# Two-layer graph attention: late mask blocks in two raw buffers with spread packs, and a preparation turned two steps behind its packing

## What is computed

```python
def _gat(x, adj, W_heads, a1, a2, W_out, b_out):          # first layer
    Wh = jnp.einsum('nf,hfd->hnd', x, W_heads)
    s1 = jnp.einsum('hnd,hd->hn', Wh, a1)
    s2 = jnp.einsum('hnd,hd->hn', Wh, a2)
    e = s1[:, :, None] + s2[:, None, :]
    e = jnp.where(e > 0, e, ALPHA * e)
    e = jnp.where(adj[None, :, :] > 0, e, NEG)
    att = jax.nn.softmax(e, axis=-1)
    hp = jax.nn.elu(jnp.einsum('hnm,hmd->hnd', att, Wh))
    feat = jnp.transpose(hp, (1, 0, 2)).reshape(N, NHEADS * NHID)
    return feat @ W_out + b_out
x = _layernorm(x + _L0_gnn_ref(...))                       # second layer: the same with 4 heads, no elu
x = _layernorm(x + _L1_gnn_ref(...))
```

## Time and profile before

| | us |
|---|---|
| median of 3 runs | 2948.03 (2943.8 to 2948.91) |
| the profiled execution | 2945.86, its span 2943.8 |
| preparation, to the first matmul of sweep 0 | 205.5 |
| sweeps 0 to 5, with the late units | 285.7 |
| PE busy over the span | 2739.7 (93%) |
| DVE, ACT, POOL busy | 1967.2 (67%), 2055.0 (70%), 571.0 (19%) |

### The profile page before, as it was taken

One profiled execution on the slowest core, in us unless ns is written; L12 is line 12 of the kernel. 1 busy time (PEld: TensorE's weight loads), 2 busy tenths in 40 slices (PEclk: granted clock), 3 DMA queues, 4 the chain that ended last, 5 costly groups with the idle time before them and its releaser, 6 DMA issues. The chain is left out here.

```text
span 2943.8 us, 62560 instructions
## 1 busy us (share of the span) xinstructions
PE 2739.7 (93%) x26702; PEld 2363.4 (80%) x26702; DVE 1967.2 (67%) x3079; ACT 2055.0 (70%) x3213; POOL 571.0 (19%) x447
## 2 busy tenths in 40 slices
PE   7986768999999999999999999999979959999997
PEld 3445656788888888888888888888868849999997
DVE  5345446877777767776777677675534458889887
ACT  4545556677777778777777877777732259999986
POOL 0021002632323323232323233130001150000000
PEclk9998989999999999999999999999989989999999
DMA  7983331111101111011011111000034344243230
GB/s 253 403 292 119 99 111 60 46 32 27 37 29 28 33 28 36 21 40 33 21 40 28 29 36 32 25 21 22 17 124 140 108 149 132 75 139 103 87 127 16
DMA packets 189144, 235.19 MB, mean 80 GB/s; under 512 B 13594, under 2 KB 113050, under 8 KB 188860
## 3 DMA queue, kind: packets, MB, share of 16 engines
q1 hardware_dynamic: 188868, 231.20, 24.4%
HBM read 180.49 MB, written 50.66 MB: 79 GB/s over the span
## 5 line engine op out<-in xcount | busy, mean ns | idle before, releaser
L419 PE MATMUL l_ps<-l_uv,l_bc 128*128 128x258 f16 x16384 | 1858.6, 275 | 85.8 <-DVE l_bc L649 81.7
L419 PEld LDWEIGHTS l_ps<-l_uv,l_bc 128*128 128x128 fp8e4 x16384 | 1602.6, 98 | 339.5 <-DVE l_bc L649 86.4
L503 ACT ACTIVATE l_bc<-l_s1b,l_kc 128x512 fp8e4<-128x512 f32 x2048 | 1281.9, 708 | 89.2 <-PE l_ps L419 89.1
L648 DVE SCALAR_TENSOR_TENSOR l_bc<-l_bc,mask_t 128x512 uint32<-128x512 uint32 x512 | 468.3, 915 | 412.5 <-ACT l_bc L503 410.0
L1016 PE MATMUL l_ps<-l_uv,l_bc 128*128 128x130 f16 x8192 | 490.9, 221 | 43.0 <-DVE l_bc L1290 41.1
L1016 PEld LDWEIGHTS l_ps<-l_uv,l_bc 128*128 128x128 fp8e4 x8192 | 485.9, 98 | 48.3 <-DVE l_bc L1290 46.7
L649 DVE TENSOR_TENSOR l_bc<-l_bc,mask_t 128x512 uint32<-128x512 uint32 x512 | 492.1, 961 | 0.0
L1109 ACT ACTIVATE l_bc<-l_s1b,l_kc 128x1024 fp8e4<-128x1024 f32 x432 | 453.4, 1141 | 0.7 <-PE l_ps L1016 0.5
L232 POOL TENSOR_TENSOR l_tu<-l_whx,l_eu 128x516 f32<-128x516 f32 x56 | 63.7, 1138 | 1225.8 <-PE l_ps L419 1223.9
L521 ACT COPY l_e<-l_ps 128x258 f32<-128x258 f32 x256 | 94.4, 369 | 260.9 <-PE l_ps L419 260.9
L654 DVE SCALAR_TENSOR_TENSOR l_e<-l_ps,l_sc,l_e 128x258 f32<-128x258 f32 x256 | 118.0, 481 | 162.0 <-ACT l_e L521 162.0
(11 more groups left out here) (152 smaller groups left out, 1399.6 us busy)
## 6 DMA issues: line engine op xcount, KB each, us to landing
l_uv<-in_adj SPq DMA_DIRECT2D x128, 512.0 KB, 6.7
l_uv<-uv SPq DMA_DIRECT2D x128, 260.0 KB, 5.4
l_s1b<-l_srow SPq DMA_DIRECT2D x64, 256.0 KB, 3.2
l_whx<-l_wh SPq DMA_DIRECT2D x64, 256.0 KB, 4.4
feat<-l_e SPq DMA_DIRECT2D x64, 256.0 KB, 2.4
l_uv<-feat SPq DMA_DIRECT2D x32, 512.0 KB, 3.7
l_wh<-l_bc SPq DMA_DIRECT2D x38, 256.0 KB, 8.0
uv<-l_uv SPq DMA_DIRECT2D x8, 1040.0 KB, 4.7
```

Of the source, the lines that this page charges most:

```text
L419: last = nc.tensor.matmul(sums(t, m), pattern(k, m).bitcast(F8)[:, j, t * P:(t + 1) * P], uv[:, slot(h, order[k]) + j, 2 * m * W1:2 * (m + ...
L503: ins = act.activation(pattern(k, 0).bitcast(F8)[:, j, :], s1b[q][:, :], ACT.Relu, bias=kc[:, h, jt:jt + 1], scale=STEEP, saturate=False)
L648: dve.scalar_tensor_tensor(c, v, ONE8X4, m, ALU.bitwise_xor, ALU.bitwise_and)
```

## The change

- Late units use two raw buffers in turn (`home(n)` is n % 2), and `load_unit(n)` waits for VectorE's pack of unit n-2 instead of n-1. Two loads are issued before sweep 0, then four in each sweep, for units two ahead.
- The packs of late units stand behind every second chunk of a sweep's eight turns (m = 1, 3, 5, 7: chunks 3, 5, 7 and the next sweep's chunk 1), on ScalarE and VectorE alike, instead of m = 1 to 4. The fourth stands right ahead of the copies of the sums.
- The second raw buffer takes the place of the four late pack buffers. Of four late units, the first two are now packed into a part of `mask_t` that is written last (4 rows of 512 bytes each), the others into the two pack buffers of preparation.
- In preparation `packed_at` begins with steps 0 and 1, so units 0 and 1 are packed on ScalarE after the copies of these steps and on VectorE ahead of `scores`; the other 38 are spread over steps 3 to 59. Every unit is turned and written two steps after its pack instead of one.
- The weights W, a1 and a2 are loaded ahead of the first part of x.

```diff
-    packed_at = [3 + n * 58 // EARLY for n in range(EARLY)]
+    packed_at = [0, 1] + [3 + n * 58 // (EARLY - 2) for n in range(EARLY - 2)]
+    turned_at = [i + 2 for i in packed_at]
...
-        late = [words[:, twin + RAW + r * PK:twin + RAW + (r + 1) * PK] for r in range(PER)]
+        late = [mask_t[:, at:at + 4, 7 * blk:8 * blk].rearrange("p (m a) (j k) -> p m a j k", m=2, k=2)
+                for at in (24, 28)]
...
+        def home(n):
+            return n % 4 if n < EARLY else n % 2
+
         def loads(n):
-            return 32 * (n // 4 + 1 if n < EARLY else EARLY // 4 + n - EARLY + 1)
-
-        def raw(n):
-            return raws[n % 4 if n < EARLY else 0].rearrange("p (m k j) -> p m k j", m=2, k=2)
+            return 32 * (n // 4 + 1 if n < EARLY else EARLY // 4 + (n - EARLY) // 2 + 1)
+
+        def raw(n, k):
+            return raws[home(n)].rearrange("p (m k a j) -> p m k a j", m=2, k=2, a=2)[:, :, k, :, :]
 
         def pair(n):
-            return (packs[n % 2] if n < EARLY else late[n % PER]).bitcast(U8).rearrange("p (m j k) -> p m j k", m=2, k=2)
+            if n >= EARLY and n % PER < 2:
+                return late[n % PER]
+            return packs[n % 2].bitcast(U8).rearrange("p (m a j k) -> p m a j k", m=2, a=2, k=2)
...
-                    sp.wait_ge(s_pd, n - 3 if n <= EARLY else n)
+                    sp.wait_ge(s_pd, n - 3 if n < EARLY + 2 else n - 1)
...
-            load_x(0)
             for k in range(KF):
                 sp.dma_start(wall[:, k, :, :], W[:, k * P:(k + 1) * P, :].rearrange("h p e -> p h e")).then_inc(s_wl, 16)
             for m, a in enumerate((a1, a2)):
                 sp.dma_start(abc[:, m, :, :], a.unsqueeze(0).to_broadcast([P, H, D])).then_inc(s_wl, 16)
-            for i in range(1, XPARTS):
+            for i in range(XPARTS):
...
-            n = EARLY
-            load_unit(n)
+            for n in range(EARLY, EARLY + 2):
+                load_unit(n)
...
-                if g < LATE:
-                    n += 1
+                ahead_of = range(EARLY + 2 + PER * g, min(EARLY + 2 + PER * (g + 1), UNITS))
+                for n in ahead_of[:1]:
                     load_unit(n)
                 if g > 0:
                     store(g - 1)
                     if g < G - 1:
                         load_mean(g + 1)
-                if g < LATE:
-                    for _ in range(PER - 1):
-                        n += 1
-                        if n < UNITS:
-                            load_unit(n)
+                for n in ahead_of[1:]:
+                    load_unit(n)
...
-                    if packed_at[n] + 1 == i:
+                    if turned_at[n] == i:
                         turn_unit(n)
...
-                act.wait_ge(s_ul[n % 4 if n < EARLY else 0], loads(n))
+                act.wait_ge(s_ul[home(n)], loads(n))
                 if 2 <= n < EARLY:
                     act.wait_ge(s_mt, n - 1)
-                if EARLY <= n < EARLY + PER:
-                    act.wait_ge(s_pd, EARLY)
+                elif EARLY <= n < EARLY + 2:
+                    act.wait_ge(s_pw, STEPS)
+                elif EARLY <= n < EARLY + PER:
+                    act.wait_ge(s_mt, EARLY)
                 elif n >= EARLY:
                     act.wait_ge(s_mt, n - PER + 1)
...
             for g in range(G):
-                for k in range(ahead, CPB):
-                    compare(g, k)
-                    if k == ahead and g > 0:
+                turns = [(g, k) for k in range(ahead, CPB)] + ([(g + 1, k) for k in range(ahead)] if g + 1 < G else [])
+                for m, (gk, k) in enumerate(turns):
+                    compare(gk, k)
+                    if m == 0 and g > 0:
                         exponentials(g - 1)
-                    if g < LATE and 2 < k < 3 + PER:
-                        pack(EARLY + PER * g + k - 3)
-                if g < G - 1:
-                    for k in range(ahead):
-                        compare(g + 1, k)
+                    if g < LATE and m % 2 == 1:
+                        pack(EARLY + PER * g + m // 2)
                 for t in range(TPB):
...
             weights()
+            for n in range(2):
+                pack(n)
             scores()
             scale_factors()
             for i in range(STEPS):
                 for n in range(EARLY):
-                    if packed_at[n] == i:
+                    if n > 1 and packed_at[n] == i:
                         pack(n)
                 for n in range(EARLY):
-                    if packed_at[n] + 1 == i:
+                    if turned_at[n] == i:
                         write_mask(n)
...
-                    if g < LATE and 1 <= m <= PER:
-                        pack(EARLY + PER * g + m - 1)
+                    if g < LATE and m % 2 == 1:
+                        pack(EARLY + PER * g + m // 2)
```

More of the change, by code:

```diff
@@ L255, in load_unit @@
                 else:
-                    sp.wait_ge(s_pd, n - 3 if n <= EARLY else n)
+                    sp.wait_ge(s_pd, n - 3 if n < EARLY + 2 else n - 1)
                 for m in range(2):
                     at = b * blk + m * 2 * P
-                    sp.dma_start(raw(n)[:, m, :, :], adj[at:at + 2 * P, c * blk:(c + 1) * blk].rearrange(
-                        "(p k) j -> p k j", k=2)).then_inc(s_ul[n % 4 if n < EARLY else 0], 16)
+                    sp.dma_start(raws[home(n)][:, m * 2 * blk:(m + 1) * 2 * blk].rearrange("p (k j) -> p k j", k=2), adj[at:at + 2 * P, c * blk:(c + 1) * blk].rearrange(
+                        "(p k) j -> p k j", k=2)).then_inc(s_ul[home(n)], 16)
             def store_step(i):
@@ L396, in turn_unit @@
                     pe.wait_ge(s_me, n - 3)
-                to, src = unit_bank(n).bitcast(BF16), pair(n).rearrange("p m j k -> p m (j k)").bitcast(BF16)
+                to, src = unit_bank(n).bitcast(BF16), pair(n).rearrange("p m a j k -> p m a (j k)").bitcast(BF16)
                 for j in range(4):
@@ L400, in turn_unit @@
                         at = (2 * j + m) * P
-                        last = nc.tensor.transpose(to[:, at:at + P], src[:, m, j * P:(j + 1) * P], ident16[:, :])
+                        last = nc.tensor.transpose(to[:, at:at + P], src[:, m, j // 2, j % 2 * P:(j % 2 + 1) * P],
+                                                   ident16[:, :])
                 last.then_inc(s_mt, 1)
@@ L479, in pack @@
             def pack(n):
-                act.wait_ge(s_ul[n % 4 if n < EARLY else 0], loads(n))
+                act.wait_ge(s_ul[home(n)], loads(n))
                 if 2 <= n < EARLY:
                     act.wait_ge(s_mt, n - 1)
-                if EARLY <= n < EARLY + PER:
-                    act.wait_ge(s_pd, EARLY)
+                elif EARLY <= n < EARLY + 2:
+                    act.wait_ge(s_pw, STEPS)
+                elif EARLY <= n < EARLY + PER:
+                    act.wait_ge(s_mt, EARLY)
                 elif n >= EARLY:
                     act.wait_ge(s_mt, n - PER + 1)
-                act.activation(pair(n).bitcast(F8)[:, :, :, 0], raw(n)[:, :, 0, :], ACT.Relu, scale=STEEP,
+                act.activation(pair(n).bitcast(F8)[:, :, :, :, 0], raw(n, 0), ACT.Relu, scale=STEEP,
                                saturate=False).then_inc(s_pa, 1)
@@ L609, in pack @@
                 dve.wait_ge(s_pa, n + 1)
-                dve.tensor_scalar(pair(n).bitcast(F8)[:, :, :, 1], raw(n)[:, :, 1, :], 0.0, 2.0, ALU.is_gt,
+                dve.tensor_scalar(pair(n).bitcast(F8)[:, :, :, :, 1], raw(n, 1), 0.0, 2.0, ALU.is_gt,
                                   ALU.subtract, saturate=False).then_inc(s_pd, 1)
```

## The result

| | before | after |
|---|---|---|
| median, us | 2948.47 | 2861.44 (2860.22 to 2865.99) |
| ratio | | 0.971 (0.9694 to 0.9727) |
| profiled span, us | 2943.8 | 2858.1 |
| preparation | 205.5 | 201.3 |
| sweep 0 | 50.4 | 47.4 |

The kernel is 87 us faster, where 96 were forecast. The rows by stage come from one profile of each kernel, and profiles of equal stages differ by a microsecond or more. Sweep 0 lasts 49.7 to 51.0 in the form of before (three profiles) and 47.2 to 48.9 in that of after (five). Sweeps 1 to 5 take 235.3 to 238.8 together in the form of before (three profiles) and 157.1 in that of after (four, taking in the kernel itself).

A forecast was written before the change was run, and what follows sets the result against it. In the late sweeps TensorE was held by VectorE's masked patterns, behind ScalarE's waits for mask loads. Savings of 77.5 + 9 + 8 = 94.5 us from 2945.86 gave 2851.4, put at 2852, range 2842 to 2862.

The forecast's parts named there:

- Sweeps 1 to 5: Late sweeps after the first: load waits go, each falls from 47.1 to 31.55 us, 77.5 us won in all.
- rival (a): Late sweeps: loads still hold ScalarE if landings stretch; 28 us less won, 2880; chance 12%.
- Sweep 0: First late sweep: three load waits go, 50.4 becomes 41.4 us, 9 us won (5 to 13).
- 4.5 us for each of four: First late sweep: VectorE's make and split of chunks 4 to 7, beside GpSimd, 4.5 us per chunk.
- the us that the clock was to give back: First late sweep, from its last group on: a clock that stays up saves one us more.
- Preparation: Stage before the sweeps: set by bytes, with ScalarE waiting for loads and stores; 8 us won (3 to 16).
- lead of 2.2 in bytes: Preparation: units 4 and 5 are loaded earlier while the queue is nearly idle; net 2.2 us won.
- slack of 2.7: End of preparation: traffic falls at about 190 while the last pack starts at 193.23; 2.7 us to win.
- 3 us of the tail: From preparation's last pack to the first sweep, 12 us: 3 of them saved by TensorE running ahead.
- can be three products ahead while ScalarE waits: End of preparation: TensorE runs ahead of a waiting ScalarE, the reason given for 3 us saved.
- Rival (b): Preparation gives nothing (store waits and low clock, or late scores); sweeps as forecast, 2860 to 2866; chance 12%.
- Rival (e): Slower: late sweeps' fourth pack, ahead of the sum copies, holds TensorE until its load lands; about 2960; chance 3%.

The follow-up runs named there:

- two_raws: The changed kernel with a sweep's four late packs back behind four neighbouring turns, two raw buffers kept: 2886.47 us, ratio 0.9792.
- spread_one: The kernel before with only the four late packs spread to every second turn, one raw buffer and old preparation kept: 2904.97 us, ratio 0.9853.
- no_pool: The changed kernel without GpSimd's operations for chunks 4 to 7 of head 0 (output of that head wrong): 2849.73 us, one run.
- turn_one: The changed kernel with early units turned one step behind their packing instead of two: 2867.45 us, ratio 0.9733.
- x_first: The changed kernel with the first part of x loaded ahead of the weights again: 2862.62 us, ratio 0.9714.
- late_only: The changed kernel with the preparation of before, so only the late part is changed: 2866.62 us, ratio 0.9726.
- early_wh: The changed kernel with head 0's chunks 4 to 7 loaded at preparation step 60 and made earlier, two of them in preparation: 2850.18 us, ratio 0.9677.
- vec_make: The changed kernel with VectorE doing all six operations of head 0's chunks 4 to 7, GpSimd only a tiny fill: 2860.07 us, ratio 0.9709.

## Why the prediction was right, and where it was not

- **Sweeps 1 to 5**: 78.2 us against 77.5, and the mechanism is the one forecast: two_raws and spread_one show that it takes both halves. The forecast was 157.8 for the five sweeps, and every profile of this form has 157.1. The layout held nearly row by row: exponentials still wait 2.60, the first evacuation is waited for by 0.82 (0.9 forecast), the period is 31.4 (31.55). The 4x256 form of the pack takes the 0.69 that I took, where GpSimd is quiet. The loads' 3 us to spare were enough, so rival (a) did not come.
- **Sweep 0**: 3.0 us against 9, outside the bounds of 5 to 13. The failed term is "4.5 us for each of four" chunks of make and split. It was 5.7, 5.8, 4.9 and 5.8, and the pack between them 1.53, from 213.66 to 237.29. That puts the last group at 36.1 instead of 31. The row of 1.53 in the earlier trace rows was there, but I mixed it with 0.7; the trace has 12 long operations of 21, and none in no_pool. The other 0.9 is the us that the clock was to give back: from the start of the last group to sweep 1 it takes 11.3, before 11.4. And 3.0 is one pair of profiles; by the means of all profiles of each form it is 2.2.
- **Preparation**: 4.2 us against 8, inside its bounds. That the queue stays at 407 and that ScalarE then waits for stores was right. The lead of 2.2 in bytes was 2.5 at unit 28, but its reason is not borne out: turn_one asks for the loads as early and packs unit 28 at 146.04, where the kernel before does at 145.97. The lead needs the later turns. The slack of 2.7 gave 0.7: the last pack came 3.2 earlier in all. The 3 us of the tail were 1: from the last pack to sweep 0 it is 11.3 us, before 12.3. The step that failed is that TensorE "can be three products ahead while ScalarE waits". It cannot, since a turn that waits for VectorE's pack stands in its queue ahead of the products: at 189.16 it had just waited 1.91 for one, with six products (10.6 us, four matmuls each in these rows) still behind it.

```profile
189.16 0.62 PE L404 MATMUL l_ps<-l_ident,l_uv 128*128 128x128 bf16 x8 [1.91 <-DVE l_uv L614]
189.62 3.65 PE L390 MATMUL l_ps<-mask_t 128*128 128x512 f32 x8
...
193.56 7.08 PE L390 MATMUL l_ps<-mask_t 128*128 128x512 f32 x16
```

- **The four wh loads** in one piece still cost a stall at 150 us; the clock fell to 0.68 there, which before came in the window after (0.66). That these four loads are what the stall comes from is argued from their place in the queue; no run moves them. **Weights ahead of x** is 0 as said (x_first). **Packs 0 and 1 ahead of the scores** were put at 0; no run takes them out alone. With the old turns they bring nothing (turn_one beside late_only); what they bring with the later ones is open.
- **The sum**: 94.5 forecast, 85.7 in the profiled execution (78.2 + 3.0 + 4.2 + 0.3). The forecast of 2852 erred by 9.4, of which 6 are in sweep 0 and 3.8 in the preparation; 0.7 went the other way in the late sweeps. So 2861.44 lies within the forecast's own range, 2842 to 2862, by 0.6 us only: the late sweeps bear the forecast out, the other two terms came to a third and a half of what was put down. Of its signs, sweep 0 of 41 us (47.4) and its start near 197 (201.3) did not come. Rival (b) named the time, 2860 to 2866, but not the cause: preparation gave half and not nothing. Rival (e)'s price is not consistent as written: each us in five sweeps makes 90 by 43 us after the start, less than the 94.5 won, so about 2942 and not 2960.
- **The Trainium skill's ceiling of 435 GB/s** (DMA: Bandwidth & Descriptors, Where 436 GB/s comes from), by which preparation would have won 16, was again not reached: of the 10 us windows of preparation none passes 408 in any of these kernels. The Trainium skill gives 435 there for the side of SBUF and says that transfers between HBM and SBUF are bound by about 358; the 400 GB/s of 60 to 140 us in the kernel after are above that, so the measured rate decides.

## What to carry to other kernels

Lay a stage out anew with measured durations, engine by engine, and look for the smallest margin at the last user, since a reserve further up does not help: that gave the late sweeps to 1%. When a wait is taken away, price the work that it hid as it runs in company and not alone. Where VectorE and GpSimd share a stage that VectorE bounds, starting that work earlier, where VectorE idles (early_wh, 11 us), is worth more than dividing it between the two, or than giving it all to VectorE (vec_make).

## What was not expected of the hardware

- A VectorE operation on 512 to 1024 elements per partition takes 0.69 us alone and 1.42 to 1.62 where it meets a GpSimd operation, in make, pack and the second operation of the split alike (the first kept its 0.68 or 0.69 each time), and two of GpSimd's three take 1.45 to 1.50 in sweep 0, where 1.04 and 1.13 are seen in the preparation. In sweep 0, six operations on VectorE alone were faster than three on each.
- What a gap costs beyond itself: 48 matmuls took 5.53 behind a gap of 1.49 (spread_one), 8.33 behind one of 4.06 (two_raws) and 7.90 behind one of 7.85 (the kernel after, 0.79 granted for 205 to 245 us; in no_pool the same stretch had 0.96). The length of the gap alone does not set it: they took 5.53 behind 2.95 (two_raws), 7.18 behind 2.15 (spread_one) and 6.78 behind 9.49 (the kernel before).
